# Layer 0's mixing product: one fp32 matmul set, or three fp32r ones from split operands

## What is computed

```python
h = layernorm(x, n1_g, n1_b)
p = h @ w_in + b_in                                  # 96 -> 192 channels
local = depthwise_conv3x3(p, k_conv)
lr, rl = ema_scan(local, axis=2), ema_scan(local, axis=2, reverse=True)
tb, bt = ema_scan(local, axis=1), ema_scan(local, axis=1, reverse=True)
mixed = 0.25 * (lr + rl + tb + bt) + local           # the mix
mixed = layernorm(mixed, on_g, on_b)
x = x + (mixed @ w_out + b_out)
x = x + gelu(layernorm(x, n2_g, n2_b) @ w1 + b1) @ w2 + b2
```

## Time and profile before

| | us |
|---|---|
| runs shown: median (lowest to highest) of 3 | 254.96 (251.88 to 255.23) |
| the profiled execution: time | 254.93 |
| its span (first to last instruction) | 253.1 |
| what lies around the span | 1.8 |
| busy: PE, DVE, ACT, POOL | 236.2, 189.4, 132.2, 124.5 |
| mean granted TensorE clock | 0.964 of full speed |

### The profile page before, as it was taken

The page is one execution under the profiler, slowest core; times in us unless marked ns, Lnnn a source line. Parts: engine busy times, 40 slices in busy tenths (PEclk is TensorE's granted clock), DMA queues, the critical chain, the costliest instruction groups (busy, mean ns, idle before and its releaser), DMA issues.

```text
span 253.1 us, 4096 instructions
## 1 busy us (share of the span) xinstructions
PE 236.2 (93%) x1366; PEld 189.2 (75%) x1366; DVE 189.4 (75%) x468; ACT 132.2 (52%) x296; POOL 124.5 (49%) x157
## 2 busy tenths in 40 slices
PE   8899759999999999998999789999999999999875
PEld 6687546969797979795878557878786878887764
DVE  5797998899999999984456678686859596777310
ACT  2676654858585856474725337263544627260620
POOL 6260577785949483839257172516253533333110
PEclk9976998999999999999999999999999999999957
DMA  6622000000000000000000000000100000100010
GB/s 160 207 69 66 1 0 0 4 0 0 3 1 0 3 1 0 3 0 0 0 4 0 0 0 3 0 31 4 34 0 31 3 31 0 34 0 32 0 34 31
DMA packets 5621, 4.99 MB, mean 20 GB/s; under 512 B 512, under 2 KB 5344, under 8 KB 5600
## 3 DMA queue, kind: packets, MB, share of 16 engines
q1 hardware_dynamic: 5168, 4.49, 5.8%
q10 hardware_dynamic: 432, 0.23, 0.4%
HBM read 3.15 MB, written 1.57 MB: 19 GB/s over the span
## 4 chain that ended last, share of the span: by engine, by line
PE 69%; DVE 15%; issue 5%; POOL 4%; ACT 4%; DMA 1%; DVEq 0%; POOLq 0%; ACTq 0%
PE bank L1050 9%; PE bank L1138 7%; PE pM L1241 7%; PE pA L1050 6%; PE pM L1006 5%; PE bank L984 5%; PE pM L989 5%; PE pM L990 4%; PE pM L991 4%; DVE cA L776 3%; DVE st L699 3%; DVE cB L776 2%; PE bank L1172 2%; POOL rs L320 2%; PE bank L1085 2%
## 5 line engine op out<-in xcount | busy, mean ns | idle before, releaser
L320 POOL TENSOR_TENSOR rs<-var,power 128x4 f32<-128x4 f32 x32 | 32.4, 1013 | 52.9 <-DVE var L703 52.7
L776 DVE SCALAR_TENSOR_TENSOR cA<-pA,cols,cA 128x528 f32<-128x528 f32 x56 | 42.3, 756 | 0.7 <-ACT cA L555 0.6
L776 DVE SCALAR_TENSOR_TENSOR cB<-bank,cols,cB 128x256 f32<-128x256 f32 x64 | 30.4, 475 | 1.4 <-ACT cB L555 1.4
L846 DVE SCALAR_TENSOR_TENSOR q<-th,bank 96x256 f32<-96x256 f32 x48 | 20.0, 417 | 11.8 <-PE bank L1050 10.9
L1241 PEld LDWEIGHTS pM<-w,hid 128*128 128x128 f32 x192 | 25.6, 201 | 1.3
L1241 PE MATMUL pM<-w,hid 128*128 128x96 f32 x192 | 25.4, 280 | 0.0
L984 PE MATMUL bank<-ident,xn 128*96 128x128 f32 x128 | 19.8, 278 | 5.9 <-POOL xn L327 3.6
L317 POOL TENSOR_TENSOR xl<-xc,xh 96x512 fp32r<-96x512 f32 x15 | 19.0, 1266 | 12.5 <-ACT xh L465 12.5
L1050 PE MATMUL pA<-q,a_half 96*96 96x256 f32 x96 | 24.8, 381 | 0.2
L1138 PE MATMUL bank<-local,mix 128*128 128x384 f32 x64 | 23.6, 514 | 0.5 <-ACT local L565 0.5
L984 PEld LDWEIGHTS bank<-ident,xn 128*96 128x96 f32 x128 | 13.9, 128 | 10.5 <-POOL xn L327 4.1
(11 more groups left out here) (205 smaller groups left out, 572.8 us busy)
## 6 DMA issues: line engine op xcount, KB each, us to landing
x_all<-in_x SPq DMA_DIRECT2D x8, 192.0 KB, 2.5
out<-y SPq DMA_DIRECT2D x8, 192.0 KB, 2.0
w<-in_w SPq DMA_DIRECT2D x1, 480.0 KB, 3.4
w<-in_w SPq DMA_DIRECT2D x1, 336.0 KB, 5.7
mix<-in_mix SPq DMA_DIRECT2D x1, 256.0 KB, 5.0
w<-in_w SPq DMA_DIRECT2D x1, 144.0 KB, 2.9
rows<-in_rows ACTq DMA_DIRECT2D x1, 144.0 KB, 5.4
w<-in_w SPq DMA_DIRECT2D x1, 96.0 KB, 5.2
```

The costliest lines, as they stand in the source:

```text
L320: pool.tensor_tensor(rs[:, :], var[:, :], power[:, :], ALU.pow).then_inc(step, 1)
L776: dve.scalar_tensor_tensor(out=acc, in0=src, scalar=col(f"k{'AB'[grp]}{k}"), in1=acc, op0=ALU.mult, op1=ALU.add).then_inc(s["conv_step"], 1)
L846: dve.scalar_tensor_tensor(out=moved(c, k + 1)[0:D, half(h)], in0=th[c % 2][0:D, half(h)], scalar=1.0, in1=step_bank(k, h), op0=ALU.add, o ...
```

## The change

The data `local` and the matrix `mix` are each split into a high part, rounded to fp32r, and a low part, the rest. The product is made as high x high + low(mix) x high(local) + high(mix) x low(local), twelve fp32r matmuls of 128 x 384 in place of four fp32 ones. ACT writes the high part from PSUM (two instructions) and then the plain copy (two instructions); POOL subtracts them (two instructions of 128 x 384), at the head of its body. PE does the eight matmuls that need no low part of the data, then waits for `local_low`, then does the last four. POOL's `xl1` (`low1`) goes behind `xl2` from body 2 on. At the start, ACT makes `mix_h` behind `setup_on`, and POOL makes `mix_l` ahead of `setup_w_out`.

```diff
@@ POOL
+            def setup_mix_low():
+                pool.wait_ge(s["mix_high"], 1)
+                pool.tensor_tensor(mix_l[:, :], mix[:, :], mix_h[:, :].bitcast(F32), ALU.subtract)\
+                    .then_inc(s["mix_low"], 1)
...
             def body0(i):
                 n, f, c, m, g = i + 2, i + 1, i, i - 1, i - 2
-                if tile_known(f) and not peeled(f, 0):
-                    pool.wait_ge(s["x1_split"], 2 * f + 2)
-                    wait(pool, s["p_psum"], 2 * f)
-                    split_low(xl1, xc1, xh1).then_inc(s["x1_lo"], 1)
+                if tile_known(m):
+                    wait(pool, s["mix_done"], 2 * m)
+                    for k in range(2):
+                        part = slice(k * 384, (k + 1) * 384)
+                        pool.wait_ge(s["local_copied"], 2 * m + k + 1)
+                        pool.tensor_tensor(local_l[:, part], local[:, part], local_h[:, part].bitcast(F32),
+                                           ALU.subtract).then_inc(s["local_low"], 1)
+
+                def low1():
+                    if tile_known(f) and not peeled(f, 0):
+                        pool.wait_ge(s["x1_split"], 2 * f + 2)
+                        wait(pool, s["p_psum"], 2 * f)
+                        split_low(xl1, xc1, xh1).then_inc(s["x1_lo"], 1)
+
+                if not tile_known(g):
+                    low1()
                 if tile_known(g):
                     pool.wait_ge(s["x2_split"], 2 * g + 2)
                     wait(pool, s["hid_psum"], 3 * g)
                     split_low(xl2, xc2, xh2).then_inc(s["x2_lo"], 1)
+                    low1()
@@ ACT
+            def setup_mix():
+                act.wait_ge(s["mix_loaded"], 16)
+                act.activation(mix_h[:, :], mix[:, :], ACT.Copy).then_inc(s["mix_high"], 1)
...
                 if tile_known(m):
+                    act.wait_ge(s["cT_done"], 2 * m + 2)
+                    wait(act, s["mix_done"], 2 * m)
                     for k in range(2):
-                        if k == 0:
-                            act.wait_ge(s["cT_done"], 2 * m + 2)
-                            wait(act, s["mix_done"], 2 * m)
+                        act.activation(local_h[:, k * 384:(k + 1) * 384], bank[4 + k][:, 0:384],
+                                       ACT.Copy).then_inc(s["local_high"], 1)
+                    wait(act, s["local_low"], 2 * m)
+                    for k in range(2):
                         act.activation(local[:, k * 384:(k + 1) * 384], bank[4 + k][:, 0:384],
-                                       ACT.Copy).then_inc(s["local_ready"], 1)
+                                       ACT.Copy).then_inc(s["local_copied"], 1)
@@ PE
-                    pe.wait_ge(s["local_ready"], 2 * m + 2)
+                    pe.wait_ge(s["local_high"], 2 * m + 2)
+                    pe.wait_ge(s["local_copied"], 2 * m + 2)
                     if peeled(i, 1):
-                        pe.wait_ge(s["mix_loaded"], 16)
+                        pe.wait_ge(s["mix_high"], 1)
+                        pe.wait_ge(s["mix_low"], 1)
+
+                    def mix_pass(a, w, v, first=False, last=False):
+                        for k in range(2):
+                            done = pe.matmul(bank[4 + a][:, 0:384],
+                                             w[:, k * TOKENS + a * P:k * TOKENS + (a + 1) * P],
+                                             v[:, k * 384:(k + 1) * 384], start=first and k == 0,
+                                             stop=last and k == 1)
+                        return done
+
                     for a in range(2):
-                        for k in range(2):
-                            last = pe.matmul(bank[4 + a][:, 0:384],
-                                             mix[:, k * TOKENS + a * P:k * TOKENS + (a + 1) * P],
-                                             local[:, k * 384:(k + 1) * 384], start=(k == 0), stop=(k == 1))
-                        last.then_inc(s["mix_done"], 1)
+                        mix_pass(a, mix_h, local_h, first=True)
+                        mix_pass(a, mix_l, local_h)
+                    pe.wait_ge(s["local_low"], 2 * m + 2)
+                    for a in range(2):
+                        mix_pass(a, mix_h, local_l, last=True).then_inc(s["mix_done"], 1)
```

More of the change, by code:

```diff
@@ L170, in build @@
         cB = [sb(f"cB{k}", TOKENS) for k in range(2)]
-        local = sb("local", 2 * 2 * INNER)
+        local, local_h, local_l = sb("local", 4 * INNER), sb("local_h", 4 * INNER, F32R), sb("local_l", 4 * INNER, F32R)
+        mix_h, mix_l = sb("mix_h", 2 * TOKENS, F32R), sb("mix_l", 2 * TOKENS, F32R)
         mixed = sb("mixed", 2 * 2 * INNER)
@@ L191, in build @@
             "x_loaded", "bn1_step", "var1_ready", "ln1_step", "xn1_ready", "trx_done", "x1_split", "x1_lo",
-            "p_psum", "tap0_done", "conv_step", "cT_done", "local_ready", "mix_done", "mixed_ready",
+            "p_psum", "tap0_done", "conv_step", "cT_done", "local_high", "local_copied", "local_low", "mix_high", "mix_low", "mix_done", "mixed_ready",
             "bnm_step", "varm_ready", "lnm_step", "mtr_done", "mc_ready", "wout_done", "xb_ready", "x2_ready",
@@ L404, in body0 @@
                     if peeled(i, 0):
+                        setup_mix_low()
                         setup_w_out()
@@ L614, in body0 @@
                     setup_on()
+                    setup_mix()
                 if peeled(i, 0):
```

## The result

| | before | after |
|---|---|---|
| all runs: median (lowest to highest) | 253.42 (251.83 to 255.23), 4 runs | 264.50 (263.10 to 265.56), 4 runs |
| ratio, 95% interval | 1 | 1.0432 [1.0325, 1.0538] |
| the profiled execution: time, span | 254.93, 253.1 | 265.56, 263.8 |
| busy: PE, DVE, ACT, POOL | 236.2, 189.4, 132.2, 124.5 | 237.6, 190.4, 138.1, 141.3 |
| mean granted TensorE clock | 0.964 | 0.953 |

Times are in us. The forecast was 260.4, with a range to 263.3: the direction was right, and the loss was about twice as large.

What follows compares the result with a forecast made beforehand. The prediction took a loop through POOL's `xl2` and PE's `mlp1` as the bound, so PE's 0.57 us saving counted for nothing. Terms 0.04 + 0.26 + 1.47 + 1.73 + 1.94 = 5.44 on 254.93 gave 260.4 us, range 256 to 263.3.

Steps and rivals of the forecast that it cites:

- the pair: POOL's two subtractions for `local_l`, ahead of `xl2`: 0.97 us each, 1.94 together.
- Bodies 7 and 8: No `xl1` to move away, so `mlp1` waits for the whole pair: +1.73 in body 7, +1.94 in body 8.
- the split mix costs PE more: Rival on PE's mix: fp32r passes dearer than their columns say, 0.1 to 0.6 us a body, 261.8 us; chance 0.08.
- PE is the bound: Rival in layer 0: PE is the bound and POOL has room, giving 254.5 us; chance 0.10.
- POOL and DVE get in each other's way: Rival in layer 0: DVE stands still during POOL's extra 1.94 us, giving 266 us; chance 0.02.
- In ACT's queue behind them stands the split of `x1`: ACT in full bodies: plain copies end about 0.8 us later, but the split behind them delays nothing; cost nothing.
- POOL's 0.49: Bodies 4 to 6: `xb` to `mlp1` grows from 3.74 to 4.23 us, +0.49 each, +1.47 together.
- the forecast hole before the last four passes: PE's mix: after eight passes PE waits for `local_low`, a hole of 0.5 us, 1.9 in bodies 7 and 8.
- the clock: Rival on PE: clock falls in the new holes, one or two stretches giving 261.8 to 263.3 us; chance 0.13.
- The start: Bodies 1 and 2: +0.35 in body 1, taken up in body 2, +0.04 left; `mix_h` and `mix_l` 0.0, bound +0.3.
- six terms smaller by 0.26: Bodies 3 to 8: with 0.84 us per POOL subtraction each term would be 0.26 smaller, the time 258.7 us.
- the first rival: Layer 0: PE is the bound and POOL has room, 254.5 us; chance 0.10.

Runs made afterwards that it cites:

- experiment 10: Changed kernel plus three zero-weight fp32 matmuls, added to the mix's own bank, in PE's wait for `local_low` in bodies 7 and 8: 262.46 us, ratio 1.0391.
- 2: Changed kernel without POOL's two subtractions, ACT's plain copies and the last four passes, so one product is left out: 253.92 us, ratio 1.0103.
- experiment 1: Changed kernel with ACT's plain copies of `local` moved behind the split of `x1`: 263.03 us, ratio 1.0452.
- 4: Kernel before plus ACT's two rounded copies to `local_h`, which nobody reads, ahead of those to `local`: 258.54 us, ratio 1.0292.
- 6: Kernel before plus two unread POOL subtractions reading two different buffers (`local`, `mix`), with `xl1` behind `xl2`: 260.71 us, ratio 1.0271.
- experiment 5: Changed kernel plus three unread fp32 matmuls of 256 columns in PE's wait for `local_low` of body 8: 263.91 us, ratio 1.0464.
- 8: Changed kernel with plain copies behind the `x1` split, `mlp1`'s `xl2` pass last in its first part, and three unread matmuls in body 8's wait: 260.27 us.
- experiment 3: Kernel before plus two unread POOL subtractions with both inputs from one buffer, and `xl1` behind `xl2`: 255.25 us, ratio 1.0176.
- the last filler: Kernel before plus two unread matmuls of ones in PE's wait in the last body of layer 1: 251.51 us, ratio 0.9972.
- 7: Changed kernel without the product with `local`'s low part, and with `mlp1`'s pass on `xl2` last in its first part: 248.86 us, ratio 0.9857.
- 12: Kernel before with its fp32 mix, only `mlp1`'s pass on `xl2` put last in its first part: 253.33 us, ratio 0.9956.

## Why the prediction was wrong

**Right, and shown.** POOL, not PE, sets what the mix's shortening is worth: bodies 4 to 6 took 13.51 with ACT's order repaired (forecast 13.50) and about 13.43 with the pair alone. The pair costs 1.98 (forecast 1.94). Bodies 7 and 8 pay it whole: +1.82 and +1.93 against 1.73 and 1.94 (experiment 10). A pass takes 0.175, so "the split mix costs PE more" falls. "PE is the bound" falls too: with POOL's pair gone (2), a shorter mix gave nothing. "POOL and DVE get in each other's way" falls: the 56 taps of the earlier trace rows now have a mean of 755 ns, against 756 before, while POOL has 17 us more work in all.

**The step that failed: ACT.** "In ACT's queue behind them stands the split of `x1`, which then ends as the transposes of `xn2` do: no loss." I had the waiting row right and saw room where there was none. The split already released the transposes before, with nothing but the 0.15 us of the handing over between them, so the copies' 0.73 arrives whole; in the loop it makes 13.74 where POOL alone makes 13.5. Beyond POOL's part it is 0.25 in each of bodies 4 to 6, which 1 and 4 show from both sides, and 0.33 in body 3, of which experiment 1 took back only 0.15; 1.1 in all. Of two delays in one loop the larger counts, not the sum: ACT's 0.74 covers POOL's 0.49, which is why the forecast hole before the last four passes does not exist and why the repair of ACT gained 0.23 a body only.

**The step that failed: the clock**, the larger part. I kept it as a rival at 0.13, with the argument that holes of 0.5 us in these bodies had left the clock at 1.00. But the holes of the change are 1.8 us there, far from that row and nearer to the 2.71 of the earlier trace rows. Body 8 paid 1.6, and layer 1's fall at 153 us 1.6 more. That the waits bring the first is shown as far as this: with work in both of them neither body falls (10), the pair alone brings the fall as well (6), and of the five profiles with a bare wait of 1.8 us in body 7 or in both (the changed kernel, 1, 5, 6, 8) each had one fall behind one of the two waits, while experiment 3, with waits of 1.49 and 1.51 us there, had none. Where only body 7's was 1.8 (1, 5, 8) the fall came behind that one; why body 7's left the clock alone in the changed kernel and in 6 is open. So is the second: it stands in the profiles of the changed kernel and of 5 and in no other, and PE's waits around it (1.17 and 0.34 us) are the same before and in 10, where the clock held.

**The start, mis-sized.** Bodies 1 and 2 were +0.70, not +0.04. At the head of body 1 ACT was 0.49 late (23.88 against 23.39): half was there from the first instructions (DVE's first statistics of the stage started at 9.46 instead of 9.20). The mix of body 1 added 0.49 (forecast 0.35), and body 2 took up 0.27, less than I counted on. Only the 0.49 of the mix is clearly the change's: experiment 5 has the same code up to body 8, and there the statistics started at 8.90, ACT was at the head of body 1 at 23.06, the mix again added 0.49, and bodies 1 and 2 ended 0.26 ahead of before. So the start differs by up to 0.9 us from one execution to the next, and a price of `mix_h` is not shown.

The sum, then: 5.44 forecast, +0.66 start, +1.09 ACT, +0.09 body 7, +3.17 clock and +0.16 in layer 1's last stretch make the 10.61 of the table. (Two small slips of the forecast change nothing in it: six terms smaller by 0.26 give 258.8 and not 258.7, and the lower bound of 256 is not half-way between 260.4 and the 254.5 of the first rival, which is 257.5.) The base had a share in the distance of the medians too: the profiled execution of before was one with the last fall of the clock, as many of its runs were not, and the changed kernel's four all ran at 0.952 to 0.954.

## What to carry to other kernels

Where several engines hand a tile round in a loop, write down for each wait by how much its releaser was early, and take the handing over out of it: here PE's transposes started 0.14 to 0.15 us behind ACT's split in every version, with a wait shown or without, so that distance was no room at all. An instruction that is put ahead of the releaser costs what is left, and the largest such delay in the loop counts, not their sum. Shortening one of two things that end together gives nothing: look for the order of work (here the pass that needs the late operand last) that lets the other move as well. Count new long waits on PE (here two of 1.8 us) as a likely fall of its clock, price it from a stretch at the lower level, and test it by putting unread work into all such waits, since the clock may fall behind any of them. A fall that lies ahead of what an edit added was not brought there by the edit.

## What was not expected of the hardware

- The same rows can run at either level of the clock. First y to last y, code that is the same in all versions without the last filler, took 86.3 to 86.6 us in eight of their profiles (before, after, 2, 4 to 7, 10) and 83.4 in four (1, 3, 8, 12). Before and experiment 3 had the same wait of 1.34 us there, and only before's clock fell behind it. That is 3 us of spread that no edit of layer 0 was meant to touch.
- POOL's subtraction of 128 x 384 took 0.98 to 1.00 us with two different input buffers and 0.83 (1.61 for the pair) when both inputs were the same buffer. An unread stand-in must read what the real instruction reads.
